# An AdaLN block with attention and a gated low-rank feed-forward: W_base turned in the attention part and kept in DRAM, and two projections of the second group moved among the first pair's rows

## The reference

```
mod = (silu(c) @ wmod) -> sa, ca, ga, sb, cb, gb ; ga and gb pushed away from 0 to at least 0.25
h = layernorm(x) * (1 + ca) + sa
q, k, v = h @ wq, h @ wk, h @ wv      # 32 heads of 32
out = softmax(causal(rope(q) rope(k)^T / sqrt(32))) v
x = x + ga * (out @ wo)
h = layernorm(x) * (1 + cb) + sb
base = h @ W_base^T + b_base
gate = softmax(h @ W_gate^T);  thr = sigmoid(h @ W_thr + b_thr) * 0.125
w = max(gate - thr, 0) normalised over 8 experts
moe = ((h @ A_w^T) weighted by w) @ B_w^T * 2      # 8 experts of rank 16
out = x + gb * (base + moe)
```

## Time and profile before

| | |
|---|---|
| runs | 1822.21, 1814.59, 1817.67 us, median 1817.67 |
| profiled execution | 1819.76 us, span of the trace 1818.0 us |
| PE busy | 1643.7 us (90%), 9459 matmuls |
| DVE, ACT, POOL busy | 1010.9 (56%), 985.4 (54%), 611.1 (34%) |
| chain that ended last | PE 63%, ACT 10%, DVE 10%, issue 8%, DMA 4%, POOL 3% |
| DMA | 174.52 MB, mean 96 GB/s |

### The profile page before, as it was taken

One profiled execution on the slowest core, in us unless ns is written; L12 is line 12 of the kernel. 1 busy time (PEld: TensorE's weight loads), 2 busy tenths in 40 slices (PEclk: granted clock), 3 DMA queues, 4 the chain that ended last, 5 costly groups with the idle time before them and its releaser, 6 DMA issues.

```text
span 1818.0 us, 29711 instructions
## 1 busy us (share of the span) xinstructions
PE 1643.7 (90%) x9459; PEld 1196.8 (66%) x9459; DVE 1010.9 (56%) x3248; ACT 985.4 (54%) x2368; POOL 611.1 (34%) x483
## 2 busy tenths in 40 slices
PE   3667989999999998899999999999879999999997
PEld 0235666666666765677667667666457888888885
DVE  1535547667576664556666666665535445445443
ACT  1333667887887776667777777777742101101110
POOL 1441424334343230423433332331322333333342
PEclk8788999999999998999999999998589999999998
DMA  9633233444443338223323323223443211211210
GB/s 338 226 135 76 74 86 91 108 122 109 129 114 77 97 77 247 57 61 96 72 68 97 71 68 97 67 60 78 119 132 93 70 59 45 70 49 56 69 48 34
DMA packets 170786, 174.52 MB, mean 96 GB/s; under 512 B 20898, under 2 KB 120562, under 8 KB 170644
## 3 DMA queue, kind: packets, MB, share of 16 engines
q1 hardware_dynamic: 166484, 164.42, 32.5%
q10 hardware_dynamic: 4160, 8.39, 1.4%
HBM read 96.68 MB, written 25.21 MB: 67 GB/s over the span
## 4 chain that ended last, share of the span: by engine, by line
PE 63%; ACT 10%; DVE 10%; issue 8%; DMA 4%; POOL 3%; SPq 2%; ACTq 0%; DVEq 0%; POOLq 0%
PE ps_s L1186 12%; PE ps_s L661 10%; PE ps_qkv L1186 9%; PE ps_pv L1254 7%; PE ps_s L1229 7%; PE ps_t L1197 6%; ACT rows_sb L1436 4%; PE ps_s L622 3%; PE ps_s L623 3%; PE ps_s L624 3%; DVE rows_sb L1657 2%; ACT probsT L1472 1%; DVE bias_m L1675 1%; PE ps_qkv L663 1%; DVE ps_s L1698 1%
## 5 line engine op out<-in xcount | busy, mean ns | idle before, releaser
L1436 ACT ACTIVATE rows_sb<-rows_sb,bias_m 128x640 f32<-128x640 f32 (+7 forms) x512 | 398.1, 778 | 228.1 <-DVE bias_m L1675 227.8
L1657 DVE CUSTOM_DVE_ANT_0 rows_sb<-ps_t,mask 128x512 f32<-128x512 f32 (+3 forms) x512 | 296.8, 586 | 157.6 <-PE ps_t L1197 150.9
L1472 ACT ACTIVATE probsT<-ps_s 128x512 f32<-128x512 f32 (+2 forms) x640 | 321.5, 549 | 13.4 <-PE ps_s L1229 12.5
L1197 PE MATMUL ps_t<-stk 96*128 96x512 f32 (+3 forms) x768 | 277.5, 366 | 45.5 <-DVE m_rows L1688 25.7
L1229 PE MATMUL ps_s<-stk 98*128 98x512 f32 (+3 forms) x768 | 238.7, 392 | 16.2 <-DMA stk<-m_rows 12.0
L1698 DVE TENSOR_TENSOR ps_s<-ps_s,mask_t 128x128 f32<-128x128 f32 (+1 forms) x384 | 121.4, 340 | 184.5 <-PE ps_s L1229 182.8
L1197 PEld LDWEIGHTS ps_t<-stk 96*128 96x128 f32 x768 | 151.8, 198 | 102.8 <-DVE m_rows L1688 36.7
L1229 PEld LDWEIGHTS ps_s<-stk 98*128 98x128 f32 x768 | 135.9, 199 | 107.6 <-issue 51.9
L1254 PE MATMUL ps_pv<-probsT,v_all 128*32 128x256 f32 (+1 forms) x2816 | 189.3, 363 | 1.3 <-ACT probsT L1472 1.3
L1822 POOL TENSOR_TENSOR rope_b<-rope_b,rope_sin 128x512 f32<-128x512 f32 x64 | 82.2, 1284 | 278.0 <-DVE rope_b L1642 278.0
L1657 DVE CUSTOM_DVE_ANT_0 rows_sb<-ps_t,mask,smax_part 128x128 f32<-128x128 f32 (+3 forms) x256 | 140.8, 550 | 49.8 <-PE ps_t L1197 23.5
(11 more groups left out here) (190 smaller groups left out, 3085.9 us busy)
## 6 DMA issues: line engine op xcount, KB each, us to landing
stk<-rot SPq DMA_DIRECT2D x384, 128.0 KB, 2.4
probsT<-in_L_wmod_dram SPq DMA_DIRECT2D x5, 2048.0 KB, 8.3
wm_one<-in_L_wmod_dram SPq DMA_DIRECT2D x5, 2048.0 KB, 9.0
w_raw<-in_L_attn_wq_dram SPq DMA_DIRECT2D x16, 512.0 KB, 4.0
w_raw<-in_L_attn_wk_dram SPq DMA_DIRECT2D x16, 512.0 KB, 4.4
w_raw<-in_L_attn_wv_dram SPq DMA_DIRECT2D x16, 512.0 KB, 4.1
attn_scratch<-attn_sb SPq DMA_DIRECT2D x128, 64.0 KB, 3.1
a_raw<-attn_scratch SPq DMA_DIRECT2D x16, 512.0 KB, 4.9
```

The source lines that it names most:

```text
L1197: pe.matmul(bank[:, 0:c1 - c0], stk[0:3 * HD, u % 2, 0, qt // 4, h, qt % 4 * P:(qt % 4 + 1) * P], stk[0:3 * HD, u % 2, 1, part, h, 0:c1 - ...
L1436: act.activation(row, row, ACT.Exp, bias=bias_m[:, qt, h:h + 1], scale=SCALE, accum_out=sums[:, qt // 4, h, qt % 4:qt % 4 + 1]).then_inc(s ...
L1472: act.activation(probsT[:, w % 4, hs[0]:hs[-1] + 1, 0:n], s_bank[(NS * u + k) % 3][:, 0:len(hs) * n].rearrange("p (h n) -> p h n", h=len(hs)),
L1657: dve.tensor_tensor_reduce(rows_sb[:, to, at + c0:at + c1], bank[:, 0:n], mask[:, BANK - n:BANK] if last else mask[:, 0:1].broadcast_to([P ...
```

## The change

1. `chains_of`: group 1 is no longer taken whole; its chains (1, 0) and (1, 1) join (0, 4) and (0, 5) in `first_rows` (`FIRST_CHAINS`), which now has 96 matmuls among 24 rows. The turned values of group 0 go to rows 7 and 15 (`FIRST_V`). ACT and POOL split group 1's query and key weights ahead of the first pair's exponentials; the rotation of (1, 0) is done right after the rows.
2. `norm_step` runs on to half period 17: in 10 to 17 a tile of W_base is loaded into `x_next`, turned in the same slots, copied by one ACT copy in place of four activations, split and stored into a second DRAM tensor, `wb_scratch`. No statistics and no normalisation are made.
3. W_base's eight pieces leave `turn_weights`, `split_weights` and `rest_weights`; three pieces are left. `wb_lo` is read (4 MB, one transfer) at the end of half period 30, `wb_hi` (4 MB) after the last scores. PE waits for both ahead of the loop.

```diff
@@ chains_of
-    whole = t == 0 or (t + 1) % G == 0
+    whole = (t + 1) % G == 0
@@ after the tables
+ROPE_AT[0, 0] = ROUND_AT[0, 2] = (1, 1)
@@ norm_step
-    if 0 <= u - LN_U < NT and i in NORM_STEPS:
+    if 0 <= u - LN_U < 2 * NT and i in NORM_STEPS and (u - LN_U < NT or NORM_STEPS[i][0] in ("turn", "split")):
@@
-LEAD = 8
-FIRST_M0, FIRST_V0 = 13, 16
+FIRST_CHAINS, LEAD = [(0, 4), (0, 5), (1, 0), (1, 1)], 8
+FIRST_M0, FIRST_V = 13, (7, 15)
@@ phase_b_tensor
-            project(0, lambda: turn_weights(0))
-            turn_weights(1)
+            project(0, turn_weights)
             def rest_and_xn():
-                turn_weights(2)
                 pe.wait_ge(st_hi, UNITS)
...
             project(1, rest_and_xn)
+            pe.wait_ge(wb_ld, 32)
             tile_loops(pe, body)
@@ SP
+            def load_wb(a, to):
+                sp.dma_start(to[:, :, :].bitcast(F32), wb_dram[a].rearrange("(k p) o -> p k o", p=P)).then_inc(wb_ld, 16)
...
-                if 0 <= u - 1 - LN_U < NT:
+                if 0 <= u - 1 - LN_U < 2 * NT:
                     store_next(u - 1 - LN_U, 1)
...
                 if u == PAIRS - 2:
                     load_a(sp, 0)
+                    sp.wait_ge(h_st, 2 * 16 * 4 * NT)
+                    sp.wait_ge(wo_lo_ok, KT)
+                    load_wb(1, wb_lo)
+            sp.wait_ge(st_ok, NS * PAIRS)
+            load_wb(0, wb_hi)
             store_attn(2 * PAIRS - 1)
             phase_b_sync(sp)
@@ first_rows
-                cuts = [LEAD + (6 * KT - LEAD) * k // NR for k in range(NR + 1)]
+                total = 3 * KT * len(FIRST_CHAINS)
+                cuts = [LEAD + (total - LEAD) * k // NR for k in range(NR + 1)]
@@ next_mod
+                if tt >= NT:
+                    act.copy(h_next[:, :], bank[:, 0:BANK]).then_inc(h_mod[half], 1)
+                    return
@@ ACT ahead of the loop
-            for i in range(5):
+            for n in range(4):
+                split_qk(1, n)
+            for i in range(4):
                 row_exps(0, i)
             copy_vT(0, 0)
...
+            round_rot(1, 0)
@@ DVE ahead of the loop
+            rope_products(1, 0)
```

More of the change, by code:

```diff
@@ L470, in adaln_block @@
         seq = {"dve": 0}
-        items = [("ag", 0), ("ag", 1), ("bt", 0)] + [("wb", o) for o in range(KT)]
+        items = [("ag", 0), ("ag", 1), ("bt", 0)]
         n_dma = {"bt": E_}
@@ L487, in piece @@
             ks = slice(4 * half, 4 * half + 4)
-            if kind == "wb":
-                return tuple(w[:, ks, k * P:(k + 1) * P] for w in (wb_hi, wb_lo))
             if kind == "bt":
@@ L496, in piece_cols, with turned @@
             return AGW - ER if (kind, k) == ("ag", 1) else P
-        parts = [slice(0, 4), slice(4, 6), slice(6, len(items))]
         turn_bank = [ps_t[0], ps_t[1], ps_qkv, ps_pv]
-        def turned(part):
-            for i, (kind, k) in list(enumerate(items))[parts[part]]:
+        def turned():
+            for i, (kind, k) in enumerate(items):
                 for half in range(2):
@@ L551, in load_early @@
             sp.wait_ge(proj_mm, 6 * T)
-            for i in range(len(stage)):
+            for i in range(len(items)):
                 load_piece(sp, i)
@@ L576, in phase_b_sync @@
             load_x(0, 0)
-            load_pieces(range(len(stage), len(items)))
             load_x(1, 1)
@@ L603, in phase_b_tensor, with turn_weights @@
             pe.transpose(ps_pv[:, 0:4 * KT], mcol_rows[:, :], ident[0:4 * KT, 0:4 * KT]).then_inc(mcol2_t, 1)
-            def turn_weights(part):
-                for n, i, kind, k, half, bank in turned(part):
+            def turn_weights():
+                for n, i, kind, k, half, bank in turned():
                     if n == 0:
@@ L722, in body, with split_weights @@
                     split_h(i + 1)
-            def split_weights(part):
-                for n, i, kind, k, half, bank in turned(part):
+            def split_weights():
+                for n, i, kind, k, half, bank in turned():
                     rows = piece_cols(kind, k)
@@ L838, in body, with rest_weights @@
                     dve.tensor_tensor(x1[:, e, cols], x1[:, e, cols], xn[:, cols], ALU.add).then_inc(last_ok, 1)
-            def rest_weights(part):
-                for n, i, kind, k, half, bank in turned(part):
+            def rest_weights():
+                for n, i, kind, k, half, bank in turned():
                     rows = piece_cols(kind, k)
@@ L949, in load_next @@
                     sp.wait_ge(ln_tr, 2 * n)
-                sp.dma_start(x_next[:, :], x_rows[n * P:(n + 1) * P, :]).then_inc(ln_x[tt % 2], 16)
+                rows = x_rows[n * P:(n + 1) * P, :] if tt < NT else W_base[(tt - NT) * P:(tt - NT + 1) * P, :]
+                sp.dma_start(x_next[:, :], rows).then_inc(ln_x[tt % 2], 16)
             def store_next(tt, half):
```

70 lines of the change are left out of this document (32 added, 38 removed).

## The result

The changed kernel takes **1822.09 us** (median of 20 runs, 1819.67 to 1829.01), the kernel before, run beside it, 1816.99 (20 runs, 1812.49 to 1826.29): a ratio of 1.0027, 95% interval 1.0014 to 1.0040. That is 2.5 to 7.3 us more, inside the 0.5% that the prediction called no change. The profiled execution took 1822.29, its span is 1820.4 (before 1818.0), so it is compared with before's as 2.4 us longer.

What follows compares the result with a forecast made beforehand. PE, busy 90%, was taken as the steady-state bound, transfers as that of half period 13. -16.5 + 8.4 + 8.5 + 10.3 - 10.6 = +0.1 us against the profiled 1819.8 (median 1817.67): forecast 1818 us, range 1806 to 1829.

Steps and rivals of the forecast that it cites:

- Term 1: First rows and half periods 0 and 1: moving projections among the rows fills waits and removes others, -16.5 us.
- The bound of -12: Smallest gain allowed for the first rows, if the new rotation wait and its slow clock cost as much as the old.
- Term 2: Half periods 10 to 17 without 13: turning W_base costs 1.2 us in each of seven, +8.4 us.
- costs the waits too: Half periods turning W_base: each tile costs batch 1's 3.2 us, +14 in all, giving 1832; chance 0.10.
- Term 3: Half period 13: ACT stands about 10.5 us for W_base's stores, slow beside its 8 MB of reads, +8.5 us.
- has room: Half period 13: the stores land before ACT needs them, so no cost there, giving 1809.5; chance 0.20.
- Term 4: End of the attention: the last m_rows wait in the queue behind the 4.19 MB read of wb_lo, +10.3 us.
- the slow rival: Large reads of wb_scratch take 20.3 us and not 10.8, delaying the last scores and the head, giving 1833; chance 0.12.
- the prediction's other estimate: Read of wb_lo by the Trainium skill's measured bandwidths: 9.9 to 12.3 us, a cost of +9.4 to +11.8.
- the first rival: End of the attention: small transfers pass large ones, so m_rows need not wait for wb_lo, giving 1807; chance 0.13.
- Term 5: Head of the feed-forward part: without W_base's pieces the loop starts earlier, -10.6 us.

Runs made afterwards that it cites:

- run 1: The kernel before with only the first rows' part of the change, W_base turned in the feed-forward part as before: 1805.23 us, ratio 0.9912 to before.
- run 10: The changed kernel with the second group's rotations taken later, around half period 0: 1816.70 us, ratio 0.9988 to before.
- run 9: The changed kernel with W_base's tile written by four scaled activations, bias and scale read from memory: 1833.25 us, ratio 1.0079 to before.
- runs 5 and 6: The changed kernel with no piece of W_base in half period 13, 1816.76 us; and with W_base's stores there issued ahead of the value weights, 1814.36 us.
- run 3: The changed kernel with the read of wb_lo issued behind the last m_rows transfer and not ahead of it: 1813.67 us, ratio 0.9967 to before.

## Why the prediction was right, and which terms were mis-sized

The forecast, no change at 1818, came out at 1822, and the mechanism behind it holds: both parts were run alone, and they cancel. That the total was met to 4 us is in part luck, as errors of 2 to 3 us in the terms stand against each other. By its steps:

- *Term 1, -16.5 forecast, -17.2 in the trace, -14.4 by the medians of run 1.* Two of its numbers were off, one each way. The first scores were to come 2.6 later and came 0.6 earlier. The count of waits was right (4.3 us of idle time went, 4.1 forecast), but the clock was left out: from the row at 162.4 on, before had 0.87 behind its wait of 5.90, and the changed kernel has 1.00. By an estimate from the windows that is 1.8 us (14.21 us busy at 0.87 are 12.4 at 1.00); the rest of the 3.2 is not accounted for. These are the windows of before, then of the changed kernel, from that row to the first scores:

```profile
162.38:181.01 18.63, 14.21 (x52) 9.59 (x53) 11.26 (x42) 10.15 (x21) 0.00 (x0) 0.87 0.16 36
```
```profile
162.56:180.42 17.86, 17.72 (x80) 14.24 (x81) 11.23 (x41) 9.03 (x19) 0.00 (x0) 1.00 0.56 134
```

  28 more recorded matmuls in less time. (Over the twelve kernels with these rows the first scores stand between 178.8 and 183.0, in the two without at 181.0. The mean of the twelve is 181.2, so the -0.6 is not sharper than 2 us, and on the mean the +2.6 was 2.4 too much.) Against it, the new wait for the rotation was named but taken at 2.9; with its clock of 0.91 it is 5.3, by run 10. The bound of -12 had been drawn for this.
- *Term 2, +8.4 forecast, +8.5.* That the two agree to 0.1 is luck. The seven half periods with a tile grew by 6.4, and 18, without one, gave the other 2.2; 10 and 18 wandered, one down and one up. Where both kernels had the same clock, a piece cost 1.4 to 1.5 (11, 16, 17), against the forecast's 1.2, and 0.7 to 0.8 in 14 and 15. With 10 and 12 taken from executions at a clock of 1.00 (35.5 for 34.7, 35.5 for 34.1) the seven come to 8.2, an estimate. That ACT's 1.52 and not PE's transposes made batch 1's tile dear is shown by run 9. The rival "costs the waits too" falls.
- *Term 3, +8.5 forecast, +11.2.* The mechanism held, by runs 5 and 6: the store lands 6.6 us behind the load (8.3 forecast), ACT stands 8.37 (10.5). The step that failed leads from ACT's wait to the half period: "PE is by then some 2 us behind ACT and gives those back". The half period did not grow by 2 less than ACT stood but by 2.8 more. Some 1.4 of these are the price of the turned tile itself, which the sum counts for seven half periods and not for 13; the other 1.4 are open. The slow clock is little of it, though PE's busy time rose by 5.2 for it. Run 3 has the same wait (ACT stands 8.71) and took 48.12 us with PE busy 31.61 at a clock of 0.75, the changed kernel 49.16 with 35.52 at 0.64. Run 1, with no piece there, took 38.59 with 32.17 at 0.69, before 37.98 with 29.43 at 0.85. So 3.9 and 2.7 us more of busy time lengthened the half period by 1.0 and 0.6. The rival "has room" falls.
- *Term 4, +10.3 forecast, +11.2 over half periods 29 to 31.* m_rows took 11.90 us and PE stood 10.40. Half period 31 grew by 14.0, and 29 and 30 together fell by 2.8. The 3.1 us of busy time in 31 are not behind the wait, since run 3 keeps them without it; with the wait gone 29 to 31 take 97.0 us, 0.4 over before. So the wait is 10.8 of the 11.2, and the 0.7 allowed for the clock was, if anything, too much. The large read took 13.1 us, 320 GB/s, between the forecast's 10.8 and the 20.3 of the slow rival (and above the 9.9 to 12.3 of the prediction's other estimate), and the head had room for it. The Trainium skill, "DMA: Bandwidth & Descriptors", section "Queues, rings and completion order", says that completion is not first in, first out per issuing engine, from which the first rival took that m_rows could pass. The same section says that each DMA engine consumes the descriptors of a ring in order, so it promises no pass where the large read fills the rings that the small transfer uses. The trace agrees with this reading: m_rows took 11.90 us behind the read, 5.19 beside it in another queue, 1.79 ahead of it. Which rings the two used, no run here shows.
- *Term 5, -10.6 forecast, -11.2.* Right to 0.6, step by step.
- *Left out: +2.2 in 2 to 9, -2.1 in the loop.* Neither is shown to be the change's. The even half periods wander by 1.9 us by the clock (below), and the loop took 430 to 432.5 in all the kernels, with and without the change.

So the terms erred by -3.2 and +2.5 (both in term 1), +0.1, +2.7, +0.9 and -0.6. The clock behind a wait is a cause of the two in term 1, not counted where a wait was removed and taken too small where one was added. For terms 3 and 4 it is not shown, and runs 1 and 3 speak against it.

## What to carry to other kernels

Price a wait of PE as its idle time and, where PE is full, the slow clock behind it, both when it is added and when it is removed: in half period 0 the clock was 2.1 of 5.3 us. Where PE has idle time anyway, do not read the longer busy time as a cost: 3.9 and 2.7 us more of it in half period 13 cost 1.0 and 0.6, and the wait in 31 went without its busy time changing. A large transfer belongs behind the small urgent one in the same queue, or into another queue; one moved line gave some 8 us (10 by the ratios) in each of two places. And work moved from a head with room into a stretch where the engine is full may gain nothing, so run the parts of a change alone: a change that measures as nothing held a version 1.3% faster.
